# Two moves in the order of a sixteen-head attention: turning the tokens and making keys and values ahead of turning the probabilities

## What is computed

```python
x = x + tanh(g_xattn[l]) * xattn_l(layernorm(x), context, ...)
x = x + tanh(g_ffn[l])   * ffn_l(layernorm(x), ...)
```

```python
qh = split_heads(q @ wq.T + bq);  kh = split_heads(k @ wk.T + bk);  vh = split_heads(v @ wv.T + bv)
corr = einsum('bhqd,bhkd->bhqk', qh, kh) / sqrt(8)
corr = where(row_mask, corr, -1e9)
prob = softmax(corr, axis=-1)
hidden = einsum('bhqk,bhkd->bhqd', prob, vh)     # heads side by side again
return hidden @ wo.T + bo
```

## Time and profile before

| | |
|---|---|
| median of three runs | 4570.37 us |
| time of the profiled execution | 4563.37 us |
| its span, first to last instruction | 4561.6 us |
| mean granted TensorE clock | 0.892 of full speed |
| layer 1's attention | about 1183 to 1521 us of the span, 64 tiles |
| busy over the span | PE 80%, DVE 63%, ACT 41%, POOL 31% |

### The profile page before, as it was taken

How to read it: one execution, slowest core, us unless ns; L and a number is a source line. 1 busy time by engine, 2 the same in 40 slices (tenths; PEclk the granted TensorE clock), 3 DMA queues, 4 the chain that set the end, 5 groups by cost and what they waited for, 6 DMA issues and landing times. The chain is left out here.

```text
span 4561.6 us, 95626 instructions
## 1 busy us (share of the span) xinstructions
PE 3651.8 (80%) x31569; PEld 2350.1 (52%) x31569; DVE 2882.0 (63%) x6293; ACT 1862.3 (41%) x3725; POOL 1395.2 (31%) x1775
## 2 busy tenths in 40 slices
PE   5676299999788497016995999787999898999897
PEld 5444145454566332015664665554666554666654
DVE  3798811111477769887886676566777544777654
ACT  1233222222477416434552222554666423666521
POOL 0676300000133005432441000005767303767500
PEclk9999599999899698558995999558999999999998
DMA  3111000000000000000110000200000000000000
GB/s 95 38 41 33 26 0 0 0 0 0 13 14 13 6 0 0 0 0 26 45 41 15 1 0 0 93 0 23 9 9 9 6 0 20 9 9 9 9 0 37
DMA packets 121910, 73.93 MB, mean 16 GB/s; under 512 B 57172, under 2 KB 117592, under 8 KB 120792
## 3 DMA queue, kind: packets, MB, share of 16 engines
q1 hardware_dynamic: 120376, 72.41, 5.7%
q10 hardware_dynamic: 1440, 0.34, 0.0%
HBM read 60.18 MB, written 4.19 MB: 14 GB/s over the span
## 5 line engine op out<-in xcount | busy, mean ns | idle before, releaser
L2179 POOL TENSOR_TENSOR la_turned<-la_turned,la_sines 128x1024 f32<-128x1024 f32 x128 | 301.9, 2359 | 694.5 <-DVE la_sines L2105 694.5
L790 DVE TENSOR_TENSOR l0f_y<-A,l0f_s 128x512 f32<-128x512 f32 x16 | 11.1, 692 | 463.4 <-PE A L757 463.4
L2173 POOL TENSOR_TENSOR la_scaled<-la_turned,la_rlen 128x1024 f32<-128x1024 f32 x128 | 243.7, 1904 | 17.1 <-POOL la_rlen L2166 13.7
L1948 PE MATMUL A<-l1f_wT,l1f_down_oq 128*128 128x128 f32 x384 | 54.5, 309 | 225.4 <-DVE l1f_down_oq L1909 225.4
L1057 POOL COPY l1x_vd<-half 128x16 f32<-128x16 f32 x8 | 1.2, 213 | 651.0 <-POOLq L47 651.0
L2403 ACT ACTIVATE gg_gate<-B,gg_b 128x512 f32<-128x512 f32 (+1 forms) x96 | 65.8, 686 | 280.8 <-PE B L2434 280.8
L2075 ACT ACTIVATE la_sq<-A 128x1024 f32<-128x1024 f32 x128 | 131.2, 1025 | 106.8 <-PE A L2225 81.9
L2097 DVE TENSOR_TENSOR la_turned<-A,la_cos 128x1024 f32<-128x1024 f32 x128 | 155.7, 1216 | 29.1 <-issue 15.0
L1948 PEld LDWEIGHTS A<-l1f_wT,l1f_down_oq 128*128 128x128 f32 x384 | 51.9, 220 | 229.0 <-DVE l1f_down_oq L1909 214.8
L2059 ACT ACTIVATE la_prob<-la_prob 128x512 f32<-128x512 f32 x128 | 80.7, 630 | 204.1 <-DVE la_prob L2118 204.1
L2115 DVE TENSOR_REDUCE la_top<-B 128x8 f32<-128x512 f32 x128 | 88.6, 692 | 108.2 <-PE B L2238 108.2
(11 more groups left out here) (447 smaller groups left out, 10680.0 us busy)
## 6 DMA issues: line engine op xcount, KB each, us to landing
memory_ctx<-in_ctx SPq DMA_DIRECT2D x128, 64.0 KB, 2.2
l2x_ctx<-in_ctx SPq DMA_DIRECT2D x128, 64.0 KB, 2.2
X<-in_x SPq DMA_DIRECT2D x4, 1024.0 KB, 8.0
gates_ctxT<-in_ctxT SPq DMA_DIRECT2D x16, 256.0 KB, 2.8
memory_ctxT<-in_ctxT SPq DMA_DIRECT2D x64, 64.0 KB, 1.8
l1x_ctxT<-in_ctxT SPq DMA_DIRECT2D x64, 64.0 KB
l2x_ctxT<-in_ctxT SPq DMA_DIRECT2D x64, 64.0 KB
l3x_ctxT<-in_ctxT SPq DMA_DIRECT2D x8, 512.0 KB, 4.2
```

The lines of the kernel that those rows point to most:

```text
L1948: last = pe.matmul(banks[j][0][:, t * P:t * P + P], oq[j][:, o, t * P:t * P + P], wT[:, 2 * F + o], start=(o == 0), stop=(o == F - 1))
L2173: pool.tensor_tensor(by_head(scaled), by_head(turned), spread_heads(rlen[j % 2][:], W3), ALU.mult)\
L2179: pool.tensor_tensor(turned[j % 2][:], turned[j % 2][:], sines[j % 2][:], ALU.add)\
```

## The change

Two functions are reordered, both for `projected=True` alone. On TensorE `turn_x(n+2)` and `make_kv(n+2)` come ahead of `turn_p(n-1)` instead of behind it. On ScalarE `copy_p(n-1)` comes behind `copy_x(n+2)`, `set_k(n+2)` and `keep_v(n+2)` instead of ahead of them. No instruction is added or removed, and no wait is changed. Layer 2 keeps its order.

```diff
@@ ScalarE, step(it, j)
                     at4(it, j, -3, copy_o)
                     if not projected:
                         at4(it, j, 2, set_q)
-                    at4(it, j, -1, copy_p)
                     if projected:
                         at4(it, j, 2, copy_x)
                         at4(it, j, 2, set_k)
                         at4(it, j, 2, keep_v)
+                    at4(it, j, -1, copy_p)
                     at4(it, j, 0, exps)
                     if projected:
                         at4(it, j, 2, set_q)
@@ TensorE, step(it, j)
                     at4(it, j, 0, scores)
                     at4(it, j, -3, turn_o)
-                    if not projected:
-                        at4(it, j, 2, turn_x)
+                    at4(it, j, 2, turn_x)
+                    if projected:
+                        at4(it, j, 2, make_kv)
                     at4(it, j, -1, turn_p)
-                    if projected:
-                        at4(it, j, 2, turn_x)
-                        at4(it, j, 2, make_kv)
                     at4(it, j, -2, mix)
                     if projected:
                         at4(it, j, 2, project_q)
```

## The result

The changed kernel takes 4783.19 us (median of four runs, 4781.27 to 4784.41), against 4567.51 of the kernel before in the same comparison: a ratio of 1.0475, 95% interval 1.0462 to 1.0489. That is 216 us slower. The forecast was slower too, but by 60 us (4627 us, range 4603 to 4675), and it missed by 156 us. The rival that named the clock had given 4710 to 4775 us, with a chance of 0.08.

The account below looks back on a forecast made before the run. It took the step as bound by TensorE's own work plus one 0.75 us wait; the new lap's terms sum to 5.87 us against 4.86, 59 laps give 59.4 us more, taken as 60: 4567 + 60 = 4627 us, range 4603 to 4675.

Parts of the forecast that it names:

- The rival that named the clock: TensorE's clock falls to 0.50 in layer 1's attention: laps of 7.2 to 8.4 us, 4710 to 4775 us, chance 0.08.
- the turns: TensorE works while ScalarE waits ahead of `keep_v`, then ScalarE works and TensorE waits ahead of `turn_x`: laps of 5.87 us.
- No change: Rival: `copy_p` fits into ScalarE's existing idle time, 1.10 us per step: 4567 us, chance 0.03.
- the faster rival: The early copy lets `project_q` follow `mix` at once, filling TensorE's pause: about 4543 us, chance 0.03.
- the sum's assumption: All terms of the 5.87 us lap in layer 1's attention were taken at full clock, 1.00.
- another stage: The stage at 180 to 230 us, cited against the clock's fall: clock 1.00 with TensorE 77% busy.
- the term from `set_q` to `turn_x`: From the end of ScalarE's `set_q` to the load of TensorE's `turn_x`: 0.07 us.
- the 1.4 us that it gave VectorE to spare: VectorE's subtraction ends 2.90 us behind `set_q`'s end and `exps` comes at 4.32, so VectorE has 1.4 us to spare.
- TensorE's terms: On TensorE, `turn_x` to what follows `make_kv` takes 0.76 us, and `turn_p` 0.87 us.
- ScalarE's terms: On ScalarE, `keep_v` to `copy_p` 0.45 us, `copy_p` to `exps` 1.00, `exps` to `set_q` 1.18, `set_q` itself 0.37.

Follow-up runs that it names:

- fillers: The changed kernel plus ten unread identity transposes per step on TensorE, six ahead of `turn_x` and four ahead of `project_q`: 4662.51 us.
- the late fillers: Four unread transposes per step ahead of `project_q` only: 4565.69 us added to the kernel before, 4685.63 us added to the changed kernel.
- Freed: The changed kernel plus ten unread transposes, with `update` no longer waiting for the `set_q` just ahead of it: 4639.60 us.
- The two halves: The kernel before with only ScalarE's order changed, 4658.29 us, and with only TensorE's order changed, 4697.35 us.
- the first (measured with fillers): The kernel before with only ScalarE's order changed, plus seven unread transposes per step on TensorE: 4600.08 us; without them 4658.29 us.
- the second: The kernel before with only TensorE's order changed, not run with added transposes: 4697.35 us.

## Why the prediction was wrong

*Right: the direction and the turns.* `keep_v` can't start before `mix` is over, `copy_p` falls behind it, and TensorE and ScalarE work in turns. "No change" and the faster rival had no basis; the idle time ahead of `keep_v`, ended by `mix` in every step, was the row that said so, and it grew from 10.1 us to 167 us in 59 steps.

*Wrong: the clock.* The step that failed is the sum's assumption that every term holds at 1.00. Its loss was written up as a rival at 0.08, on the ground that another stage kept 1.00 with 77% busy. The runs show 121 us for it: 4783.19 of the changed kernel against 4662.51 with fillers, and no gain from the late fillers where the clock is up. The rival's arithmetic was near: laps of 7.2 to 8.4 us, 8.45 measured. That nearness is in part luck: it took the clock as lost for good, while the windows show it back at 1.00 for a few us 23 times in 59 laps, and it left out the wait below, and the two errors go against each other. The other stage was a poor witness: its pauses were of 0.5 to 0.6 us (0.56 and 0.51 in the lap at 200 us), those of the changed order up to 1.3. But length alone does not decide: with the late fillers pauses of 1.3 us stood beside a clock of 0.96. The Trainium skill (TensorE: Matmul & The Clock Gate, section A second HAM failure mode) tells of another kernel in which short, frequent pauses between groups of matmuls make the clock swing; the trace agrees, with 0.50 at 1405 and 1.00 at 1408 us of one lap.

*Wrong: the term from `set_q` to `turn_x`, 0.07 us.* It was taken from the second step of the stage, where no tile was far enough for an `update`. In a full step `turn_x(n+2)` also waits for `update(n-4)`, and that for `set_q(n+1)`. The list of `turn_x`'s waits ahead of the prediction names `normed_x` and `q_set` and leaves out the third, which the kernel has: `added` of tile m-6, counted up by `update`. The prediction even expected `update` to wait about 2 us for `set_q`, and it did (2.02 in the timeline of the changed kernel), but it did not follow that wait on to `turn_x`; the 1.4 us that it gave VectorE to spare were counted to `exps`. From the end of `set_q` to `turn_x` it took 0.55 us (1407.67 to 1408.22). Freed, the lap lost 0.42: 25 us in 59 laps.

*Mis-sized: TensorE's terms.* `turn_x` to `turn_p` took 0.86 and not 0.76, `turn_p` to `mix` 1.03 and not 0.87, together 0.26 more.

*Mis-sized: ScalarE's terms.* `keep_v` to `copy_p` 0.58 (0.45 forecast), `copy_p` to `exps` 0.90 (1.00), `exps` to `set_q` 1.06 (1.18), with `set_q` 0.36: 0.10 less together. The overlap of 0.1 us does hold in front of `exps` and `set_q`, as the Trainium skill (ScalarE: Activation LUTs, section What ACT_TABLE_LOAD costs) says of activations that follow each other; I set that rule aside for rows that did not contradict it. In the row that gave 1.00 ahead of `exps`, the subtraction that `exps` needs ended at 1512.05, and `exps` started at 1512.07: it had waited for VectorE and not for the copy.

```profile
1510.82 1.23 DVE L1106 TENSOR_TENSOR l1x_prob<-A,l1x_top 128x1024 f32<-128x1024 f32 x1
```

What `set_q` waited for in its row is not shown. The overlap does not hold behind the two copies of `keep_v`, each over 64 partitions: they take 0.55 us, and `copy_p` starts 0.58 behind their start.

The account per lap at full clock: 5.87 forecast, + 0.48 + 0.26 - 0.10 = 6.51; the lap of the filled kernel shown above has 6.50, and the mean is 6.53. In us: 60 forecast, 95 measured at full clock (4662.51 against 4567.35), and 121 for the clock, 216 in all. Of the 121, 113 lie in the 59 laps (8.45 against 6.53), and most of the rest in the last steps.

*Open.* The two halves add up to nearly the whole, 91 + 130 against 216. Their waits do: 33 us for the first (measured with fillers), and for the second an estimate of 59 x (6.0 - 4.86) = 67 from its laps at full clock, 100 together, where the pair has 95. That the clock's shares add up as well, 58 and some 63 against 121, may be chance. What exactly decides whether the clock falls in a pause was not isolated.

## What to carry to other kernels

A move in a queue that is nearly in balance is judged by the longest loop through all engines, and every wait of each instruction in the loop has to be followed to its end, also those that never showed in the trace because something longer covered them. Where a change adds pauses to TensorE, work out the time at both levels of its clock and don't trust the busy share, which stays high while the clock falls. A few unread transposes in the pauses tell the two losses apart in one run, and a lap at full clock in the trace, where there is one, does it without any.

## What the runs showed of the hardware

Added work made a kernel faster: ten useless transposes per step took 121 us off 4783. Six of them, in one place, were enough for a clock of 0.99 between 1214 and 1500 us, and four in the other for 0.96.

In the changed kernel the clock rose from 0.50 to 1.00 and fell again 23 times in 59 laps of 8.45 us, with pauses of 1.3 us at most on TensorE, and was at 0.50 for 79% of the time. With the late fillers pauses of the same length stayed, and the clock was at 0.50 in 12% of the windows of 0.5 us.

In the new order the transposes of `turn_p` (weights of 128 columns) come directly behind matmuls with weights of 64 columns, and `mix` (64 columns) directly behind the transposes. From `turn_x` to `turn_p` TensorE took 0.10 us more than from `turn_x` to `mix` in the old order (0.86 against 0.76), and from `turn_p` to `mix` 0.16 more than from `turn_p` to `turn_x` (1.03 against 0.87), with 0.17 us of "issue" ahead of `mix`. That the change of width is the cause was not tested.
